# One dense tap by spans of six rows, float32 scores in row groups of 32, and no trips to HBM: attention and deformable convolution on one core

## What is computed

```
# layer 0: attention over all positions of an image
xn = group_norm(x, 32 groups) * w + b
q, k, v = split(einsum('bchw,oc->bohw', xn, qkv_w) + qkv_b)      # 4 heads of 32 channels
attn = softmax(q @ k.T * 32 ** -0.5)                             # 4096 x 4096 per head
x = proj(attn @ v) + x
# layer 1: deformable convolution, 8 groups of 16 channels, 9 taps
offset_feat = conv1x1(concat([x, 2 * feat_s]))
om = conv3x3(offset_feat) + b_om                # offsets y, x and a mask for 8 x 9 samples
val = bilinear(feat_s at (y, x), 4 corners) * sigmoid(mask)
out = relu(einsum('bgckhw,ogck->bohw', val, W_dcn) + b_dcn) + x
```

## Time and profile before

| | |
|---|---|
| median of 3 runs | 12791.58 us (12790.51 to 12822.48) |
| time of the profiled execution | 12790.43 us |
| its span | 12788.6 us |
| granted TensorE clock, mean | 0.819 |
| busy, share of the span: POOL | 10703.5 us, 84% |
| PE | 8894.0 us, 70% |
| DVE | 7910.4 us, 62% |
| ACT | 2914.1 us, 23% |

### The profile page before, as it was taken

The page is one execution under the profiler, slowest core; times in us unless marked ns, Lnnn a source line. Parts: engine busy times, 40 slices in busy tenths (PEclk is TensorE's granted clock), DMA queues, the critical chain, the costliest instruction groups (busy, mean ns, idle before and its releaser), DMA issues. The chain is left out here.

```text
span 12788.6 us, 126443 instructions
## 1 busy us (share of the span) xinstructions
PE 8894.0 (70%) x34036; PEld 3273.8 (26%) x34036; DVE 7910.4 (62%) x9169; ACT 2914.1 (23%) x3357; POOL 10703.5 (84%) x24581
## 2 busy tenths in 40 slices
PE   5666778765777767777666777766687766778732
PEld 1222222222222222222222222222232222222211
DVE  3466666666666666656666656666566666656633
ACT  2222222211222211222122222211222221222200
POOL 0488888887888888888788888888788888888888
PEclk8888888887888887888788888878788887888865
DMA  3222211112111111111211111111211111111111
GB/s 94 75 65 67 78 29 25 28 29 61 29 32 28 28 28 29 29 29 31 54 35 29 29 27 27 28 28 29 62 24 34 29 28 29 29 29 25 28 24 23
DMA packets 458806, 469.41 MB, mean 37 GB/s; under 512 B 150432, under 2 KB 274464, under 8 KB 458016
## 3 DMA queue, kind: packets, MB, share of 16 engines
q0 software_dynamic: 262144, 268.96, 10.3%
q1 hardware_dynamic: 97952, 119.95, 3.5%
q10 hardware_dynamic: 97920, 71.35, 1.8%
HBM read 390.46 MB, written 69.21 MB: 36 GB/s over the span
## 5 line engine op out<-in xcount | busy, mean ns | idle before, releaser
L408 POOL DMA_INDIRECT g<-patches,idx x8192 | 7862.1, 960 | 1254.6 <-issue 1180.1
L404 POOL TENSOR_TENSOR carrier<-carrier 128x1 f32<-128x1 f32 x15872 | 2766.3, 203 | 140.1
L982 DVE TENSOR_TENSOR ring<-ring,hats 128x1024 f32<-128x1024 f32 x1024 | 1259.3, 1230 | 2520.4 <-PE ring L655 2187.3
L494 ACT ACTIVATE p<-ring 128x1024 f32<-128x1024 f32 x2048 | 2089.2, 1022 | 2812.3 <-PE ring L622 1936.6
L597 PE MATMUL ring<-k,q 128*128 128x512 bf16 x4096 | 1763.9, 529 | 1216.2 <-DVE mx L844 796.3
L844 DVE TENSOR_REDUCE mx<-ring 128x1 f32<-128x1024 f32 x2048 | 2381.1, 1218 | 300.9 <-PE ring L597 300.9
L621 PE MATMUL ring<-q,k 128*128 128x512 bf16 x4096 | 1598.3, 390 | 307.3 <-ACT p L494 84.0
L622 PE MATMUL ring<-q,k 67*128 67x512 bf16 x4096 | 1584.9, 387 | 0.0
L655 PE MATMUL ring<-fx,hats 64*128 64x512 f32 x4096 | 1203.2, 666 | 230.8 <-ACT hats L482 178.8
L984 DVE TENSOR_REDUCE dval<-ring 128x16 f32<-128x1024 f32 x1024 | 1254.1, 1225 | 35.4
L678 PE MATMUL ps_a<-p,v 128*64 128x512 f32 x4096 | 1110.9, 621 | 2.0 <-ACT p L494 2.0
(11 more groups left out here) (117 smaller groups left out, 5707.2 us busy)
## 6 DMA issues: line engine op xcount, KB each, us to landing
g<-patches,idx POOLq DMA_INDIRECT x8192
patch_in<-in_fpad ACTq DMA_DIRECT2D x544, 64.0 KB
patches<-patch_out ACTq DMA_DIRECT2D x136, 256.0 KB
k<-k_parts SPq DMA_DIRECT2D x96, 256.0 KB
q<-q_parts SPq DMA_DIRECT2D x192, 128.0 KB
k_parts<-v SPq DMA_DIRECT2D x16, 768.0 KB
q_parts<-p SPq DMA_DIRECT2D x32, 384.0 KB, 2.6
p<-in_x SPq DMA_DIRECT2D x4, 2048.0 KB
```

The source lines that it names most:

```text
L404: last = nc.gpsimd.tensor_tensor(carrier[:, col:col + 1], carrier[:, 0:1], carrier[:, 0:1], ALU.add)
L408: nc.gpsimd.indirect_dma_start(out=g[:, part, j - CUTS[part] * GROUPS, :], out_offset=None, in_=patches[b], in_offset=bass.IndirectOffsetO ...
L494: nc.scalar.activation(p[:, n % 4, :, :], ring[u % 2][:, :, :], ACT.Exp, scale=SCALE)\
L982: then(V.tensor_tensor(cells, cells, hy[:, at * HEIGHT:(at + 1) * HEIGHT].unsqueeze(2).to_broadcast([128, HEIGHT, GC]), ALU.mult))
```

## The change

**Dense tap.** The image `fx` is now held as spans: for each of 13 blocks of 5 rows, six rows, two at a time on 64 + 64 partitions (`PAIRS` = 3). A tile's work is cut into two sets of 4 groups and each set into two halves. For each set PE makes distances of both axes (8 matmuls), ACT makes one hat of the columns and three of the row pairs (4 passes of 512 and 2 of 1024), and a new DVE operation, `weigh_hats`, multiplies the three row hats with the column hat: 1536 elements in place, both operands in SBUF. For each half PE runs 6 matmuls of 128 rows and 208 columns into `half_set`, a PSUM bank of its own (`ps_x1`) outside the ring, and DVE picks the block (`chosen`) and reduces 2 x 208 elements.

**Samples.** The bank `ps_x0` now holds `turned` (384 columns) and `aligned` (128). The bilinear weights `w4` move to a tile in SBUF, `weights`. `align` runs once for each tile, with 9 matmuls in a row, and PE then waits for the relu, whose result goes to SBUF (`relu_out`).

**Scores.** q and k stay in SBUF: float32 (`qf`, `kf`) and two bf16 parts. A score is one float32 matmul of 32 rows for each head, the four heads in four row groups, and one bf16 matmul that adds the maximum from `mq`. For the maxima each ring use takes two heads (two row groups) and three bf16 products instead of one matmul of 128 rows for one head.

**Trips.** `k_parts` and `q_parts`, their DMAs and waits are gone. In `project` the product with `fs_s` moves ahead of the wait for the attention's output. POOL's program keeps its instructions; the gathers' destination is written as one tile.

```diff
-USE_D = DENSE * (2 + GROUPS)
+USE_D = 2 * DENSE
...
+SETS = 2 * DENSE
+SET_GROUPS = GROUPS // 2
+SET_AT = tuple(i * KT_TILE // SETS for i in range(SETS))
+BLOCK = 5
+BLOCKS = -(-HEIGHT // BLOCK)
+PAIRS = (BLOCK + 1) // 2
...
-        k1 = sb("k1", [128, HEADS, N], bf16)
-        k2 = sb("k2", [67, HEADS, N], bf16)
+        kf = sb("kf", [128, N])
...
+        qf = sb("qf", [128, QB])
+        k_high, k_low = sb("k_high", [128, N], bf16), sb("k_low", [128, N], bf16)
+        q_high, q_low = sb("q_high", [128, QB], bf16), sb("q_low", [128, QB], bf16)
...
-        g = sb("g", [128, PARTS, 2 * GROUPS, PATCH])
+        g = sb("g", [128, PICKS, PATCH])
...
+        weights, relu_out = sb("weights", [128, 8 * GROUPS]), sb("relu_out", [128, 128])
...
-        turned, aligned = ps_x[0], ps_x[1][:, 0:128]
+        turned, aligned, half_set = ps_x[0][:, 0:384], ps_x[0][:, 384:512], ps_x[1]
...
-                    sp.dma_start(k_parts[:, :, n].rearrange("a c n -> c a n"), k_made).then_inc(k_spilled, 16)
-                    sp.wait_ge(k_spilled, b * (16 * USE_K) + 16 * (c + 1))
...
-                    nc.scalar.activation(k_made[:, 0, :], ring[u % 2][:, :, :].rearrange("p i n -> p (i n)"), ACT.Identity,
-                                         bias=k_bias).then_inc(k_high, 1)
+                    for made in (kf, k_high):
+                        last = nc.scalar.activation(made[:, c * 1024:(c + 1) * 1024], ring[u % 2][:, :, :].rearrange("p i n -> p (i n)"),
+                                                    ACT.Identity, bias=k_bias)
+                    last.then_inc(ring_free[u % 2], 1)
...
+                nc.scalar.activation(made[:, 0, :], ring[k % 2][:, 0, :], ACT.Abs, bias=plus_x, scale=-1.0)
+                for pair in range(PAIRS):
+                    last = nc.scalar.activation(made[:, 1 + pair, :], ring[k % 2][:, 1, :], ACT.Abs, bias=pair_rows[:, pair:pair + 1],
+                                                scale=-1.0)
...
+                            for n, (q_part, k_part) in enumerate(((q_high, k_high), (q_high, k_low), (q_low, k_high))):
+                                for i in range(2):
+                                    rows = slice((2 * pair + i) * HD, (2 * pair + i + 1) * HD)
+                                    last = mm(ring[u % 2][:, i, :], q_part[rows, sub * 128:(sub + 1) * 128],
+                                              k_part[rows, c * 512:(c + 1) * 512], start=n == 0, stop=n == 2)
...
+                        mm(ring[u % 2][:, i, :], kf[rows, n], qf[rows, :], start=True, stop=False)
...
+                        last = mm(ring[u % 2][:, i, :], ones_b[rows, :], mq[rows, :], start=False, stop=True)
...
+                    for pair in range(PAIRS):
+                        last = mm(cells, hats[:, i % 2, 1 + pair, j * 128:(j + 1) * 128], fx[:, pair, :, group * GC:(group + 1) * GC],
+                                  start=pair == 0, stop=pair == PAIRS - 1)
...
-                split(then, ring[0][:, 0, :], q_bias, q_made, q_rest).then_inc(ring_free[0], 1)
+                wait_slot_read(dve, before_att(s, b, 0), 0)
+                V.tensor_sub(q_low[:, :], qf[:, :], q_high[:, :]).then_inc(q_ready, 1)
...
-                w4 = turned[:, 512 - 4 * (j1 - j0):512]
+                w4 = weights[:, 0:4 * (j1 - j0)]
...
-                V.tensor_add(feat_old[:, first:first + 128], feat_old[:, first:first + 128], aligned).then_inc(relu_used, 1)
...
+                V.tensor_add(feat_old[:, first:first + 128], feat_old[:, first:first + 128], relu_out[:, :]).then_inc(relu_used, 1)
...
+            def weigh_hats(s, b, t, i):
+
+                dve.wait_ge(hats_ready, tile_number(s - 1, t) * SETS + i + 1)
+                made = hats[:, i % 2, :, :]
+                V.tensor_tensor(made[:, 1:, :], made[:, 1:, :], made[:, 0:1, :].to_broadcast([128, PAIRS, SET_GROUPS * 128]), ALU.mult)\
+                    .then_inc(hats_weighed, 1)
```

More of the change, by code:

```diff
@@ L42 @@
 PARTS = 4
-CUTS = tuple(min(2 * part, PICKED) for part in range(PARTS + 1))
+CUTS = tuple(min(2 * part, PICKED - (PARTS - part)) for part in range(PARTS + 1))
 LAST_TAPS = CUTS[PARTS] - CUTS[PARTS - 1] + DENSE
-USE_D = DENSE * (2 + GROUPS)
+USE_D = 2 * DENSE
 KT_TILE = KT // SUB
@@ new lines, in head, with make_hats @@
+                nc.scalar.activation(qf[:, :], ring[0][:, 0, :], ACT.Identity, bias=q_bias)
+                nc.scalar.activation(q_high[:, :], ring[0][:, 0, :], ACT.Identity, bias=q_bias).then_inc(ring_free[0], 1)
+            def make_hats(s, b, t, i):
+                k = hat_use(s, t, i)
+                wait_slot_full(act, before_att(s, b, k), k)
+                made = hats[:, i % 2, :, :]
[3 more added lines that the diff above has]
+                                                scale=-1.0)
+                last.then_inc(ring_free[k % 2], 1)
+                wait_slot_read(act, before_att(s, b, k), k)
+                for half in range(2):
+                    part = made[:, 2 * half:2 * half + 2, :].rearrange("p v n -> p (v n)")
+                    last = nc.scalar.activation(part, part, ACT.Relu, bias=ones_s[:, 0:1], scale=-1.0)
+                last.then_inc(hats_ready, 1)
@@ L669, in weigh, with dense_work @@
+            def dense_work(s, b, kt, fresh):
+                for t, i in hats_at(s, kt):
+                    distances(s, b, t, i)
+                for t, i, half in sets_at(s, kt):
+                    blocks_of_half(s, b, t, i, half, fresh)
             def weigh(s, b, kt):
@@ L1027, in step @@
                     for t in dense_tiles(s):
-                        for j in range(GROUPS):
-                            dense_group(s, b, t, j)
+                        for i in range(SETS):
+                            weigh_hats(s, b, t, i)
+                            for half in range(2):
+                                dense_half(s, b, t, i, half)
                         for part in range(PARTS):
```

396 lines of the change are left out of this document (176 added, 220 removed).

## The result

The changed kernel takes 13282.54 us (median; 13277.5 to 13285.81), the kernel before 12794.35 us. The ratio is 1.0376, with a 95% interval of 1.0358 to 1.0394: 488 us, 3.8% slower. The forecast was 13310 us, in 13000 to 13750. Beside the first four the kernel before took 12793.31 us and beside the next four 12791.80, so the times of these eight are compared with the 13282.54 us above. Beside the last four it took 13053 to 13446 us, and their times are compared with little but each other.

A forecast was written before the change was run, and what follows sets the result against it. POOL's own cadence was taken to bound the kernel before and after. First indices 347 + cadence 12107 + holds 740 + waits 105 + last part 11.5 + 1.8 = 13312 us, forecast 13310 us, range 13000 to 13750.

The forecast's parts named there:

- last part: End of the span after POOL's busy and idle time: 11.5 us, as in the kernel before.
- Term 2: POOL's cadence of 8192 gathers: 12107 us plus 740 us because DVE operations with both operands in SBUF hold POOL.
- the price of L962: 512 products with weights in SBUF hold POOL: 256 at 0.72 us and 256 at 0.95 us, 427 us.
- The products of the hats: weigh_hats, two for each of 128 tiles, 1536 elements: each costs POOL 1.25 us, 320 us together.
- Term 1: POOL's wait for the first indices, through prepare(0) and step 0: from 390.5 to 347 us (330 to 375).
- term 3: POOL's waits for DVE to free gather buffer, at pipeline start and batch changes: 105 us (20 to 200).
- a cover of 22 to 51: Slack in us a step: other engines need 350 to 379 us against POOL's 401.5, so POOL stays the bound.
- The maxima: Maxima stage of a step, 90.5 us before: 90 to 98 us, with matmuls 0.22 us apart.
- The loop: Loop over key tiles in a step, 199.7 us before: 195 to 216 us after.
- Rival 1: L962's operation doesn't hold POOL, so only starts and waits gain: 12570 us, 1.7% faster; chance 0.08.
- rival 2: DVE operations hold only POOL's additions, not gathers: 516 us instead of 740, 13090 us; chance 0.10.
- Rival 3: PE becomes the bound as 32-row matmuls don't run side by side: step 468 us, 15360 us; chance 0.07.

The follow-up runs named there:

- the first four: First of three groups of the twelve follow-up runs, each group on a chip of its own; the kernel before took 12793.31 us beside it.
- the next four: Second of three groups of the twelve follow-up runs, on another chip; the kernel before took 12791.80 us beside it.
- the last four: Changed kernel on a third chip, fewer POOL additions, some with weights in PSUM or maxima from upper bf16 parts: 16552.75, 17033.26, 15812.45, 16509.4 us.
- alone in the kernel before: Kernel before with only the bilinear weights of all 512 products of L962 moved from PSUM to SBUF: 13172.32 us, ratio 1.0296.
- undone in the changed one: Changed kernel with weights of parts 1 to 3 in PSUM: 13084.55 us; with hat products cut to 3 x 8 elements: 12985.75; both: 12762.07.
- doubled: Changed kernel with each of the 256 products of hats in weigh_hats done twice: 13654.03 us.
- With one addition: One POOL addition behind each gather instead of two: changed kernel 12249.17 us, kernel before 12348.83 us.
- the short maxima: Changed kernel, one addition behind each gather, maxima from upper bf16 parts alone (2 matmuls instead of 6): 12114.36 us, ratio 0.9469 to kernel before.

## Why the prediction was right, step by step

| term | predicted | measured |
|---|---|---|
| 1, first indices | 347 | 356.8 |
| 2, cadence | 12107.1 + 740 = 12847 | 13264.1 - 356.8 - 137.2 = 12770.1 (+663) |
| 3, waits for `val` | 105 | 137.2 |
| last part | 11.5 | 14.3 |

13264.1 is POOL's busy and idle time together (11365.0 + 1253.3 + 142.6 + 503.2).

**The bound.** It was POOL, before and after. The slack of the other engines was real: 1303 us less work of VectorE bought nothing.

**Term 2.** The mechanism was read rightly from two rows of `prepare`, and it is shown from both sides: alone in the kernel before (+379 us), undone in the changed one (-198, -297, together -520), doubled (+371). The size was 12% too high. The step at fault is the price of L962, 427 us for 512 products, where the trace of the changed kernel has 332 us. I took half of the products as waited, at 0.95 us, and the others as starting at a random moment, at 0.72. Waited were 238, at 0.89 us, and the 274 others cost 0.44 each. For these "a random moment" is what failed. In the kernel before with the weights in SBUF, products that had not waited cost 0.70, close to my 0.72. In the changed kernel those that began during one of POOL's gathers (141) cost 0.45 us those during an addition (55) 0.90, and those while POOL stood between two instructions (78) 0.12; why so many fall on the cheap moments there isn't shown. The products of the hats were right at 312 us against 320. The two make 644 us, of 662 by which POOL's busy time grew.

**Term 1** was short by 10 us, and **term 3** by 32, both within their ranges. In term 1 two parts were off: the first matmul of the maxima comes 49 us earlier (57.1 us instead of 105.7), not 37, and from there to the first indices it takes 15 us more, not 6 less, as the maxima of step 0 are 17 us longer too. Together with the last part, 45 us too little, they make good a part of the 77 us too much of term 2; the forecast was 28 us off.

**The other engines.** I said 350 to 379 us a step, and a cover of 22 to 51. With one addition the changed kernel's step is at most 362, so the bound held, and the inner steps got no shorter by the short maxima. Inside it two stages were mis-sized against each other. The maxima were given 7.5 us more at most, and took 18 more. The granted clock in the stage is 0.50, TensorE's lower level, where it was 0.73 in before; there a pair of matmuls in two row groups starts each 0.43 us, as the rows show:

```profile
3151.26 0.63 PE L598 MATMUL ring<-k_low,q_high 32*128 32x512 bf16 x2
3151.68 0.63 PE L598 MATMUL ring<-k_high,q_low 32*128 32x512 bf16 x2
3152.11 0.63 PE L598 MATMUL ring<-k_high,q_high 32*128 32x512 bf16 x2
3152.36 2.51 DVE L841 TENSOR_REDUCE mx<-ring 128x2 f32<-128x1024 f32 x2 [0.43 <-PE ring L598]
```

Three pairs take 1.28 us, a little more than VectorE's reduction of 1.22. I had used 0.22 us, the distance in the loop, where the granted clock is 0.99. The loop, given 195 to 216 us, took 178.9 from the first score to the last weighing with one addition; which part of my sum was too high wasn't looked into.

**Rival 1** (no price) and **rival 2** (additions only) fell with the single rows: both kinds of instruction take 1.8 us where they are held. The rule of the Trainium skill, "SBUF — State Buffer", section "Who interferes with whom", that descriptor generation goes on beside such an operation, isn't what the rows show here: the issue of an indirect gather took 1.84 us beside L962 and 0.95 beside the same product with its weights in PSUM. The section calls its reason inferred. The gather also has `idx`, a tile in SBUF, as an operand; whether it is held for reading that or for making descriptors, no run separates.

**Rival 3** (32-row matmuls not side by side) fell with the scores of one key tile:

```profile
3248.14 1.14 PE L655 MATMUL ring<-qf,kf 32*128 32x512 f32 x8
```

These are four float32 matmuls (two records each) in four row groups: 1.14 us, where one of full height took 0.99.

## What to carry to other kernels

When VectorE gets a product with both operands in SBUF, count it on POOL too, if POOL has work: an instruction of POOL that is due while it runs starts only when it is nearly through. Here 64 numbers a partition, the smaller of the two operands, decided it: in PSUM they cost POOL nothing, in SBUF some 0.65 to 0.85 us for each product of 1.23. So the memory of a scratch tile is part of the schedule. And before counting what a change saves on engines that wait, relieve the engine they wait for: here the same change is 3.8% slower with POOL's pacing additions as they were, and 0.8% faster with half of them.

## What the runs showed of the hardware

An operation of VectorE that reads both operands from SBUF holds POOL's additions and its indirect gathers that start beside it: they end as if they had started 0.13 to 0.16 us before its own end (1.10 of 1.23 us, 1.62 of 1.76 us). A gather that is already running isn't slowed: 202 of them run into an L962 of the changed kernel and take 0.960 us in the mean. With one operand in PSUM it holds neither (384 products, none with a price). The price is not tied to bf16 operands or to a cast. A TensorE stage made of 32-row bf16 matmuls in pairs was granted the lower clock level for nearly all of its 103 us (0.50 to 0.52), with PE busy 93 us of them, where the 128-row stage that it replaced was granted 0.73 with PE busy 56 us of 84.
